# A time-warping wave swept from both corners of its table at once, joined by sums in the middle

## The reference

```
x = x + tanh(g_xattn[0]) * align(ctx, layernorm(x))        # dynamic time warping
x = x + tanh(g_ffn[0])   * moe_64_experts_top_8(layernorm(x))
x = x + tanh(g_xattn[1]) * attention_16_heads(layernorm(x), ctx, ctx)
x = x + tanh(g_ffn[1])   * moe_8_experts_top_2(layernorm(x))
```

```
D = sqrt(max(aa + bb - 2 * small @ large.T, 0))          # 77 x 512 for each batch
R[i, j] = D[i, j] + min(R[i-1, j], R[i, j-1], R[i-1, j-1])
# from R[76, 511] back to R[0, 0]: each step to the least of diagonal, up, left
expanded[j] += small[i]        for every cell (i, j) of that path
```

## Time and profile before

| | us |
|---|---|
| runs | 797.85, 796.64, 796.64 |
| median | 796.64 |
| span of the profiled execution | 794.8 |
| median less that span | 1.8 |
| VectorE busy in the span | 610.5 |
| TensorE busy in the span | 658.4 |

### The profile page before, as it was taken

One profiled execution on the slowest core, in us unless ns is written; L12 is line 12 of the kernel. 1 busy time (PEld: TensorE's weight loads), 2 busy tenths in 40 slices (PEclk: granted clock), 3 DMA queues, 4 the chain that ended last, 5 costly groups with the idle time before them and its releaser, 6 DMA issues.

```text
span 794.8 us, 13507 instructions
## 1 busy us (share of the span) xinstructions
PE 658.4 (83%) x3446; PEld 499.5 (63%) x3446; DVE 610.5 (77%) x2037; ACT 397.0 (50%) x702; POOL 395.5 (50%) x399
## 2 busy tenths in 40 slices
PE   5653330188999999999999969998799999999995
PEld 2321110176787787877878846665678787877884
DVE  5799999687777777777777785688877777777774
ACT  5533110044565565555565644545456565565653
POOL 4047870036566666665666653000155666656663
PEclk9655555559999999999999975999799999999999
DMA  5424442205877677786776600000146765666761
GB/s 145 78 66 133 137 124 44 47 1 122 153 162 147 139 160 140 147 156 135 158 153 129 134 1 1 2 2 12 37 84 136 161 153 131 159 149 136 160 134 53
DMA packets 73810, 85.90 MB, mean 108 GB/s; under 512 B 39097, under 2 KB 51754, under 8 KB 70760
## 3 DMA queue, kind: packets, MB, share of 16 engines
q1 hardware_dynamic: 66714, 75.05, 44.7%
q0 software_dynamic: 4320, 9.68, 4.1%
q10 hardware_dynamic: 2734, 0.69, 0.4%
HBM read 76.69 MB, written 8.70 MB: 107 GB/s over the span
## 4 chain that ended last, share of the span: by engine, by line
PE 67%; DVE 23%; issue 5%; ACT 2%; DMA 2%; POOL 1%; DVEq 0%; SPq 0%; POOLq 0%; ACTq 0%
PE bank L1034 7%; PE bank L1035 7%; PE bank L1036 7%; PE bank_quad L1190 7%; PE bank_pair L1036 7%; PE bank_pair L1034 7%; PE bank_pair L1035 7%; PE bank_quad L1187 6%; PE bank_quad L1188 6%; DVE arena L1491 3%; PE bank_pair L1083 2%; DVE arena L1487 2%; PE bank L1126 2%; DVE arena L1445 2%; DVE arena L1435 2%
## 5 line engine op out<-in xcount | busy, mean ns | idle before, releaser
L695 POOL TENSOR_TENSOR act_lo<-arena,act_hi 128x512 fp32r<-128x512 f32 x232 | 300.5, 1295 | 193.6 <-ACT act_hi L868 190.8
L1724 DVE TENSOR_TENSOR bank_pair<-arena,bank_pair 128x512 f32<-128x512 f32 x220 | 152.5, 693 | 103.9 <-ACT arena L882 72.9
L882 ACT ACTIVATE arena<-bank 128x512 f32<-128x512 f32 x232 | 139.0, 599 | 185.6 <-PE bank L1036 185.6
L1732 DVE TENSOR_TENSOR arena<-bank_pair,arena 128x512 f32<-128x512 f32 x220 | 152.1, 691 | 16.7 <-DMA arena<-scr_mask 4.5
L868 ACT ACTIVATE act_hi<-arena 128x512 fp32r<-128x512 f32 x232 | 144.6, 623 | 12.8 <-DVE arena L1722 7.1
L1034 PE MATMUL bank_pair<-xn_hi,w_hi 128*128 128x512 f32 x232 | 92.6, 399 | 2.9 <-DVE arena L1722 2.1
L1190 PE MATMUL bank_quad<-act_lo,w_hi 128*128 128x512 f32 x232 | 92.5, 399 | 3.0 <-POOL act_lo L695 3.0
L1034 PE MATMUL bank<-xn_hi,w_hi 128*128 128x512 f32 x232 | 93.8, 404 | 0.1
L1035 PE MATMUL bank<-xn_hi,w_lo 128*128 128x512 f32 x232 | 92.6, 399 | 0.0
L1036 PE MATMUL bank<-xn_lo,w_hi 128*128 128x512 f32 x232 | 92.5, 399 | 0.0
L1036 PE MATMUL bank_pair<-xn_lo,w_hi 128*128 128x512 f32 x232 | 92.3, 398 | 0.0
(11 more groups left out here) (220 smaller groups left out, 1072.6 us busy)
## 6 DMA issues: line engine op xcount, KB each, us to landing
arena<-scr_mask SPq DMA_DIRECT2D x94, 512.0 KB, 6.7
scr_w<-prep_out POOLq DMA_DIRECT2D x25, 192.0 KB, 2.2
w_raw<-scr_w SPq DMA_DIRECT2D x25, 192.0 KB, 6.3
w_raw<-in_L_ffn_expert_gate_k SPq DMA_DIRECT2D x32, 64.0 KB, 5.9
w_raw<-in_L_ffn_expert_up_k SPq DMA_DIRECT2D x32, 64.0 KB, 5.7
w_raw<-in_L_ffn_expert_down_k SPq DMA_DIRECT2D x64, 32.0 KB, 5.2
prep_in<-in_L_ffn_wg POOLq DMA_DIRECT2D x21, 64.0 KB, 2.3
prep_in<-in_L_ffn_wu POOLq DMA_DIRECT2D x21, 64.0 KB, 2.1
```

The source lines that it names most:

```text
L695: nc.gpsimd.tensor_tensor(act_lo[:, k % 2, :], act_a[:, k % 2, :], act_hi[:, k % 2, :].bitcast(F32), ALU.subtract).then_inc(FF[f]["alo"], 1)
L882: nc.scalar.activation(act_s[:, k % 2, :], ps[4 + k % 2][:], ACT.Silu).then_inc(FF[f]["silu"], 1)
L1724: nc.vector.tensor_tensor(ps[6 + i][:], act_s[:, i, :], ps[6 + i][:], ALU.mult).then_inc(FF[f]["t"], 1)
L1732: nc.vector.tensor_tensor(act_a[:, i, :], ps[6 + i][:], mask[:, j, 512 * k:512 * (k + 1)], ALU.mult).then_inc(FF[f]["act"], 1)
```

## The change

The wave starts in both corners of each table at once. The upper half (context rows 0 to 38) is swept from the first corner, the lower half (rows 76 to 38, in reverse, with the columns in reverse) from the last, on 64 partitions each: lane 64d + 16b + c. There are 15 chunks of 35 columns (525, of which 512 count), HALF = 39 rows and SLOTS = 39 + 15 - 1 = 53.

- The lower half's context rows are read in reverse by a DRAM to DRAM copy (`scr_ctx`) and a load, both on ScalarE's queue. Two memsets on POOL clear the unused rows of `ctx_sb` first, and SP's context load waits for these.
- `distances` makes two products for each one before: one into partitions 0 to 63, one into 64 to 102 with the columns reversed.
- Where the halves meet (slot 38 onward), the two comparisons of a slot become `scalar_tensor_tensor` with a value from a table for each lane (`valid`), 14 times and 15 times.
- TensorE forms the sums of the two halves in the meeting row, chunk by chunk (`meet`), in four parts behind groups 9, 10, 11 and 12 of the weight preparation. Part c waits for the scan of slot 38 + c. VectorE takes the greatest of the negated sums (`max`, `max_index`), TensorE spreads its column to the lanes, and the wave backward starts there in both halves (`meeting`).
- `cells` becomes two instructions, partitions 0 to 63 and 64 to 127, the second with the columns reversed.
- `store_path` makes one DMA for each half and part, `load_path` four.
- The loads of the weight preparation move from POOL's queue to SP's: groups 0 and 1 ahead of the clearing of `scr_d`, the others behind `load_lanes` and ahead of `store_path`. Two of the lane loads are on ScalarE's queue. The value projections stand behind groups 0 to 11, one pair of products each, and the copies from them to `vbd` behind groups 16 to 21.

The diff, cut to its core:

```diff
-    CH = 16
-    CW = S // CH
-    SLOTS = KEYS + CH - 1
-    LANES = [32 * b for b in range(B)]
+    CH, CW = 15, 35
+    HALF = (KEYS + 1) // 2
+    LOWER = KEYS - HALF
+    DROWS = [slice(0, HALF), slice(64, 64 + HALF)]
+    SLOTS = HALF + CH - 1
+    MEET = HALF - 1
+    LSLOT = 64 + SLOTS
+    MEET_PARTS, VALUE_AT = {9: range(0, 4), 10: range(4, 8), 11: range(8, 12), 12: range(12, CH)}, 16
...
-        ON_PARTS = [(44, SLOTS), (12, 44), (0, 12)]
+        ON_PARTS = [(25, SLOTS), (5, 25), (0, 5)]
...
+        def load_path(engine, part, d):
+            first, last = ON_PARTS[part][0], (HALF, LOWER)[d] if part == 0 else ON_PARTS[part][1]
+            engine.wait_ge(s_onst[d], 16 * (part + 1))
             for b in range(B):
...
+                engine.dma_start(cells if d == 0 else cells[:, ::-1, :],
+                                 at(scr_on[d, b], first * CW,
+                                    [[CW, last - first], [ON_LANE + CW, CH], [1, CW]])).then_inc(s_path[d], 16)
...
         def _(sp):
             for b in range(B):
                 sp.dma_start(x_res[:, TPB * b:TPB * (b + 1), :], x_t[b]).then_inc(s_x[b], 16)
                 if b == 0:
-                    sp.dma_start(ctx_sb[:], ctx_1024.rearrange("b k d -> k b d")).then_inc(s_ctx, 16)
+                    sp.wait_ge(s_cz, 2)
+                    sp.dma_start(ctx_sb[0:HALF], ctx_1024[:, 0:HALF].rearrange("b k d -> k b d")).then_inc(s_ctx, 16)
...
+            for g in range(2):
+                load_prep(sp, g, *prep_span(g))
             sp.wait_ge(s_blank, 1)
...
+            for b in (2, 3):
+                load_lanes(sp, 0, b)
+            for g in range(2, GROUPS[1]):
+                load_prep(sp, g, *prep_span(g))
             for part in range(len(ON_PARTS)):
...
+                store_path(sp, part, 0)
+                load_path(sp, part, 0)
...
         def _(pool):
+            for p0 in (32, 96):
+                nc.gpsimd.memset(ctx_sb[p0:p0 + 32], 0.0).then_inc(s_cz, 1)
+            pool.wait_ge(s_cz, 2)
...
         def _(act):
+            act.dma_start(scr_ctx, at(ctx_1024, (KEYS - 1) * H, [[KEYS * H, B], [-H, LOWER], [1, H]])).then_inc(s_crev, 16)
             act.wait_ge(s_pool, 2)
             nc.scalar.activation(root_one[:], ones[:, 0:1], ACT.Sqrt)
             nc.scalar.activation(dl, ones[:, 0:CW].unsqueeze(1).broadcast_to([P, SLOTS, CW]), ACT.Copy, scale=0.0).then_inc(s_blank, 1)
+            act.wait_ge(s_cz, 2)
+            act.wait_ge(s_crev, 16)
+            act.dma_start(ctx_sb[64:64 + LOWER], scr_ctx.rearrange("b k d -> k b d")).then_inc(s_ctx, 16)
             norm(0)
...
         def _(pe):
-            pe.wait_ge(s_ctx, 16)
+            pe.wait_ge(s_ctx, 32)
...
             def distances(b):
...
+                top, bottom = dist_bank(b)[0:64, :], dist_bank(b)[DROWS[1], :]
+                nc.tensor.matmul(top, ctxT_neg[:, b, 0:64], xT0[:, b, :], start=True, stop=False)
+                nc.tensor.matmul(bottom, ctxT_neg[:, b, DROWS[1]], xT0[:, b, ::-1], start=True, stop=False)
                 pe.wait_ge(s_sq, b + 1)
+                nc.tensor.matmul(top, ones[:, 0:64], sq[:, b % 2, :], start=False, stop=True)
+                nc.tensor.matmul(bottom, ones[:, 0:HALF], sq[:, b % 2, ::-1], start=False, stop=True).then_inc(s_ab, 1)
...
+            def meet(c):
+                pe.wait_ge(s_scan, MEET + c + 1)
+                n, first = columns(c), CW * c
+                sums = ps[0][0:B, :]
+                nc.tensor.matmul(sums[:, first:first + n], meet_pick[:, 0, c, :], rst[:, MEET + c + 1, 1:1 + n],
+                                 start=c == 0, stop=False, skip_group_check=True)
+                nc.tensor.matmul(sums[:, S - first - n:S - first], meet_pick[:, 1, c, :], mst[:, (MEET + c) % MST, 0:n][:, ::-1],
+                                 start=False, stop=c == CH - 1, skip_group_check=True).then_inc(s_meet, 1)
...
                 mm.then_inc(s_pt, 1)
+                if g < RCH * B:
+                    project_values(g // B, g % B)
+                if g in MEET_PARTS:
+                    for c in MEET_PARTS[g]:
+                        meet(c)
+                if g == max(MEET_PARTS):
+                    pe.wait_ge(s_mcol, 1)
+                    nc.tensor.matmul(ps[0][:, 0:1], meet_batch[:], meet_col[:], start=True, stop=True).then_inc(s_mrep, 1)
...
             pe.wait_ge(s_r1, 1)
+            for d in range(2):
+                pe.wait_ge(s_path[d], 16 * B * len(ON_PARTS))
...
             def left_steps(s):
...
+                if s < MEET:
+                    nc.vector.tensor_tensor(lg[:, s, 0, :], left, least, ALU.is_lt).then_inc(s_steps, 1)
+                else:
+                    nc.vector.scalar_tensor_tensor(lg[:, s, 0, :], left, valid(LEFT_VALID, s), least, ALU.mult,
+                                                   ALU.is_lt).then_inc(s_steps, 1)
...
             def cells(g):
...
+                for d in range(2):
+                    half = slice(64 * d, 64 * (d + 1))
+                    out_half = on[half, s0:s1, :] if d == 0 else on[half, s0:s1, ::-1]
+                    nc.vector.tensor_tensor(out_half, ent[half, s0:s1, :], qex[half, s0:s1, 1:CW + 1], ALU.subtract).then_inc(s_on, 1)
+            def meeting():
+                dve.wait_ge(s_meet, CH)
+                done(nc.vector.max(meet_top[:], ps[0][0:B, :]))
+                settle()
+                done(nc.vector.max_index(meet_index[:], meet_top[:], ps[0][0:B, :]))
+                settle()
+                nc.vector.tensor_copy(meet_col[:], meet_index[:, 0:1]).then_inc(s_mcol, 1)
+                dve.wait_ge(s_steps, SLOTS)
+                thresholds(SLOTS - AHEAD, SLOTS)
+                dve.wait_ge(s_pool, POOL_CONST)
+                dve.wait_ge(s_mrep, 1)
+                done(nc.vector.tensor_scalar(qex[:, SLOTS, :], lane_columns[:], ps[0][:, 0:1], None, ALU.is_le))
```

More of the change, by code:

```diff
@@ L410, in prep_rows @@
             return found
[L412 to L422, removed]
-            engine.dma_start(dl[LANES[b]:LANES[b] + CH, first:last].rearrange("c s w -> c (s w)"),
-                             scr_d[b, :, first:last].rearrange("c s w -> c (s w)")).then_inc(s_dld[part][b], 16)
@@ new lines, in load_lanes, with lanes_laid, store_path @@
+        def load_lanes(engine, d, b):
+            engine.wait_ge(s_dst[b], 32)
+            first = FIRST_SLOT[d]
+            engine.dma_start(dl[lanes(d, b)].rearrange("c s w -> c (s w)"),
+                             scr_d[b, :, first:first + SLOTS].rearrange("c s w -> c (s w)")).then_inc(s_dld, 16)
+        def lanes_laid(engine):
+            engine.wait_ge(s_dld, 16 * 2 * B)
+        def store_path(engine, part, d):
+            first, last = ON_PARTS[part]
+            engine.wait_ge(s_on, 2 * ON_PIECES[part])
+            engine.dma_start(scr_on[d, :, :, first:last, :].rearrange("b c s w -> (b c) (s w)"),
+                             on[64 * d:64 * (d + 1), first:last].rearrange("c s w -> c (s w)")).then_inc(s_onst[d], 16)
@@ new lines, in load_prep @@
+        def load_prep(engine, g, r0, r1):
+            j = g % 2
+            if g >= 2:
+                engine.wait_ge(s_pt, g - 1)
+            if r1 - r0 < P:
+                engine.wait_ge(s_pzero, 1)
+            for rows, m, src in prep_rows(r0, r1):
+                engine.dma_start(prep_in[rows, j, P * m:P * (m + 1)], src).then_inc(s_pin[j], 16)
+            at_row = 0
+            for e, i, n in pieces(r0, r1):
+                wd = swd1 if e < 0 else wd1[e]
+                engine.dma_start(prep_in[:, j, DOWN + at_row:DOWN + at_row + n], wd[:, i:i + n]).then_inc(s_pin[j], 16)
+                at_row += n
@@ L844, in _ @@
             for part in range(len(ON_PARTS)):
-                for b in range(B // 2, B):
-                    store_path(act, part, b)
-                for b in range(B // 2, B):
-                    load_path(act, part, b)
+                store_path(act, part, 1)
+                load_path(act, part, 1)
             def scores0(b):
@@ L1499, in _ @@
             dve.wait_ge(s_exit, SLOTS)
-            entries(SLOTS // PIECE - 1)
-            cells(SLOTS // PIECE - 1)
+            for g in range((SLOTS - 3) // PIECE, len(PIECES)):
+                entries(g)
+                cells(g)
             first_lo(0)
```

300 lines of the change are left out of this document (171 added, 129 removed).

## The result

The changed kernel takes 773.7 us (median of 4 runs, 772.2 to 774.5) against 797.05 us for the kernel before: a ratio of 0.9707, 95% interval [0.9693, 0.9721]. It is 23.3 us faster. The forecast was 763.4 us and the range ended at 771, so the direction was right and the time came out 10.3 us too long, outside the range. The profiled execution took 773.22 us with a span of 771.5 us.

A forecast was written before the change was run, and what follows sets the result against it. VectorE's wave alone was taken to set the time up to the path: 23.3 us saved forward and 17.9 backward, minus 1.6 at the start, 4.3 meeting and 2.0 tail, 33.2 us less, giving 763.4 us (range 756 to 771).

The forecast's parts named there:

- forward: Wave forward on VectorE: 53 slots take 34.5 us (32.6 to 37), ending at 70.6 us.
- meeting: Between the waves: VectorE waits 2.3 us (0 to 5) for TensorE's sums, then 2.9 us (2.2 to 4) to the backward start.
- backward: Wave backward on VectorE: 41.0 us (35 to 44), of which 6.4 us for `cells` as two instructions that don't overlap.
- tail: From the wave's end to TensorE starting on the path: 6.7 us (5.4 to 9), against 4.7 before.
- the lanes go through DRAM: Before the first slot: lanes stored and loaded in 15 rows of 53 slots add 0.6 us (0 to 2).
- The context's load: At the start: copy, blanking and load of the reversed context rows before TensorE may start add 0.4 us (0 to 2.5).
- The blocks that POOL clears: At the start: clearing two blocks of 512 columns delays the context and x loads, costing 0.6 us.
- doubled products: Distances on TensorE: twice as many products, the two halves side by side, cost 0 (0 to 5) us.
- the first rival (no holding): Wave backward: the halves of `cells` overlap as two plain instructions, gain 3.4 us more, 758 to 760; 12%.
- A late start: Before the first slot: products run in turn or reversed context comes late, 3 to 7 us later, 766 to 771; 18%.
- the engine rule: Reversed context load: 38 rows are spread over 2 DMA engines, estimated at 1 to 2 us more.
- The weights' end: Weight preparation: TensorE reaches the path only after group 24, 780 at 5.4 us a group, over 797 from 6.8; 3%.

The follow-up runs named there:

- f1: The changed kernel with lanes in DRAM at a pitch of 192 bytes, each piece written whole: 769.29 us, ratio 0.9648.
- g1: f1 with the lane loads in two parts, slots 0 to 23 first, the rest waited for at slot 24: 766.65 us, ratio 0.9648.
- h3: g1 with e3's path parts, 39 rows of reversed context and whole 160-byte pieces for 192: 761.29 us, ratio 0.9551.
- h4: h3 with the lower half's chunks reversed where the load reads DRAM instead of where it writes SBUF: 761.78 us, ratio 0.9557.
- e3: The changed kernel with the path stored in parts from slots 25, 13 and 0 instead of 25, 5 and 0: 772.39 us, ratio 0.9693.
- f6: The changed kernel with one subtraction for `cells` instead of two, leaving out the lower half's column reversal: 771.22 us, ratio 0.9675.
- f2: The changed kernel with all lane loads issued behind the last store, pitch still 140 bytes: 776.62 us, ratio 0.9747.

## Why the prediction was off

The terms, measured less predicted, in the profiled execution: first slot +11.7, forward -0.5, meeting -2.1, backward -1.1, tail +5.2, behind the aligned sums -3.2. Together +9.9 us of span. Two terms were forecast too low, by 16.9 us together, and four too high, by 6.9, which hid part of it. The 3.2 us behind the aligned sums are luck: that stretch scatters by as much from one execution to the next.

- **The failing step is "the lanes go through DRAM".** It put 0.6 us (0 to 2) on the turnaround of before; measured are 11.0 (14.94 for 3.97). I counted rows, slots and bytes, and not where a piece of 35 columns starts. Going to f1 takes 5.8 us of it back (grid and whole pieces), the split load of g1 2.4, the shorter pitch of h3 0.6. Some 2 us over the kernel before are left (5.9 to 6.0). In h4's trace 1.5 of them lie in the store (3.3 us from the issue of the first of its two DMAs to landing, for 1.79) and 0.4 in the load (2.40 for 1.98); why is open. My bound of 2 us came from rows of the kernel before, all of them of 128-byte pieces at 128-byte steps; by them the price could not be seen.
- **The context's load** was 0.4 us (0 to 2.5) and cost 2.3 (reciprocal at 12.30 for 9.95 us), inside its bounds; about 1.2 of them go with the odd 39th row. The blocks that POOL clears were given 0.6 us by way of the x loads and cost nothing that shows. The doubled products cost nothing, as forecast.
- **The tail** was 6.7 us (5.4 to 9) and is 11.85. I charged the issues of the last part alone. I looked at no due time for the part before it, ready 2.3 us ahead of the last with four loads of its own behind it (3.12 us), and took 0.4 us a load where the reversed ones take 0.78. e3 takes the part before out of the way (3.05 us less), h4 takes the dear issues off (0.8 less); at 8.03 us the tail is then inside my 5.4 to 9.
- **The meeting** was to cost 2.3 us of waiting and costs 0.16: a pair of sums takes 0.23 us for my 0.45, so after its 2.76 us stand at `meet(0)` TensorE catches up behind group 10. The 2.9 us behind it were 2.7.
- **Forward and backward** were right within 0.5 and 1.1 us, and so was their mechanism: f6 takes back 5.3 us of the 6.4 that I charged to `cells` (the single `cells` that it keeps costs 0.08 us a time over a plain slot, which is about the rest), so the first rival (no holding) is out. The rule of the Trainium skill ("VectorE: DVE Perf Modes", section on two Vector instructions with no wait between them), which speaks against this edit, agrees with f6.
- **The rivals.** "A late start" happened and went beyond its 3 to 7 us, but not by its mechanisms: the doubled products cost nothing, and the engine rule 1.2 us. The weights' end decided nothing: 111 us, 7 later than I said, for a path at 125.
- The shift was carried to the end well enough: 634.8 us behind the aligned sums for 638.0, and the other kernels scatter over the same 4 us.

## What to carry to other kernels

When a change alters the width of a tile that is stored to DRAM in small pieces, work out where each piece starts and ends there, and pad the pitch to a boundary (16 bytes were enough here) and write the padding along. When a wave's last stretch is cut into parts, list for each part when it is ready, and count the full store, wait and load issues of the one before: the last part queues behind them. Wait only for what the first step reads.

## What was not expected of the hardware

- A store of 585 pieces of 140 bytes that start at any multiple of 4 bytes landed 7.3 us after its issue, with starts 12 bytes off a boundary 7.45, on a 64-byte boundary 5.3; whole pieces of 144 to 192 bytes on 16-byte boundaries landed in 3.0 to 4.5. The Trainium skill ("DMA: Bandwidth & Descriptors", Specifications) says that transfers below 512 bytes lose the full rate to a read-modify-write. All pieces here are below that, and the difference between 7.3 and 3.9 us is one of where they start and end, which that size alone doesn't tell.
- Issued without gaps, eight such stores ended 11.56 us after the last was issued (f2), though spread out the last took 7.3.
- A DMA whose SBUF side runs over its chunks with a negative step took 0.73 to 0.85 us to issue, with the negative step on the side of DRAM 0.42, as without one.
